# Two residual convolution layers on one core: six held chunks, a sixth tap row on PE, a first image counted from twelve buffers

## The reference

```python
# layer 0: x1 = x + conv0(gn(x))
s = z1*(1-dy)*(1-dx) + z2*(1-dy)*dx + z3*dy*(1-dx) + z4*dy*dx   # per-channel shift by under one pixel
x = x + einsum('bchw,oc->bohw', s * w_dw, w_pw)
# layer 1: out = x1 + conv1(gn(x1))
ll, lh, hl, hh = haar_dwt(x)                                     # 128x128 each
h = gelu(batchnorm(conv1x1(concatenate([ll, lh, hl, hh]), w_c1, b_c1)))   # 512 -> 128 channels
res = h
o = layernorm_chw(dwconv3x3(h, dw_w, dw_b))
o = conv1x1(gelu(conv1x1(o, pw1_w, pw1_b)), pw2_w, pw2_b)
h = gelu(batchnorm(conv1x1(o + res, w_c2, b_c2)))                # 128 -> 512 channels
out = x + haar_idwt(h)                                           # four bands back to 256x256
```

## Time and profile before

| | |
|---|---|
| median of 3 runs | 5391.47 us (5389.53 to 5392.61) |
| profiled execution | 5390.27 us, of it a span of 5388.6 us |
| busy share of the span | PE 86%, DVE 86%, ACT 80%, POOL 21% |
| counting of image 0 | 0 to 119 us |
| first pass, 8 images | 119 to 2694 us |
| c1 of image 7 | 2705 to 2822 us |
| middle | 2826 to about 4000 us |
| output | to the end |

### The profile page before, as it was taken

The page is one execution under the profiler, slowest core; times in us unless marked ns, Lnnn a source line. Parts: engine busy times, 40 slices in busy tenths (PEclk is TensorE's granted clock), DMA queues, the critical chain, the costliest instruction groups (busy, mean ns, idle before and its releaser), DMA issues.

```text
span 5388.6 us, 54861 instructions
## 1 busy us (share of the span) xinstructions
PE 4658.9 (86%) x12356; PEld 2109.0 (39%) x12356; DVE 4638.6 (86%) x4206; ACT 4333.2 (80%) x6474; POOL 1154.0 (21%) x855
## 2 busy tenths in 40 slices
PE   0889999999999999999999999999987777777775
PEld 0333334344343443444434555555642222222222
DVE  6999899898998989999808999999659888888887
ACT  4888888888788888888837888888569888888887
POOL 0000000000000000000006888888401111111111
PEclk6999999999999999999999999999999999999998
DMA  8999999999999999999973333333149999999999
GB/s 348 351 355 378 426 402 424 425 401 426 390 424 424 396 426 399 426 395 360 375 281 102 130 129 130 128 131 128 63 96 223 236 235 236 236 236 236 236 236 224
DMA packets 251726, 1562.84 MB, mean 290 GB/s; under 512 B 29744, under 2 KB 30128, under 8 KB 91824
## 3 DMA queue, kind: packets, MB, share of 16 engines
q1 hardware_dynamic: 159408, 957.11, 45.5%
q0 software_dynamic: 36864, 268.45, 24.0%
q10 hardware_dynamic: 55296, 335.57, 14.9%
HBM read 898.32 MB, written 662.70 MB: 290 GB/s over the span
## 4 chain that ended last, share of the span: by engine, by line
DMA 19%; PE 11%; DVE 10%; issue 7%; ACT 3%; POOLq 0%; DVEq 0%; POOL 0%; ACTq 0%
DMA out_x<-arena 19%; PE ps L954 4%; DVE arena L1352 3%; DVE arena L1376 2%; PE ps L880 2%; ACT arena L821 2%; PE ps L1001 2%; DVE arena L1489 2%; DVE ps L1365 2%; PE ps L961 1%; PE ps L973 1%; PE ps L985 1%; DVE arena L1481 0%; DVE arena L1480 0%; ACT arena L814 0%
## 5 line engine op out<-in xcount | busy, mean ns | idle before, releaser
L1056 PE MATMUL ps<-arena,c2T 128*128 128x512 f32 x2048 | 1025.2, 652 | 366.8 <-ACT arena L814 364.5
L880 PE MATMUL ps<-arena 128*128 128x512 f32 x2048 | 985.1, 626 | 58.7 <-DMA arena<-out_x 41.3
L864 PE MATMUL ps<-arena 128*128 128x512 f32 x2048 | 967.8, 600 | 44.6 <-DVE arena L1275 23.9
L814 ACT ACTIVATE arena<-ps,small 128x512 f32<-128x512 f32 x1024 | 713.7, 779 | 97.7 <-DVE arena L1481 90.4
L1056 PEld LDWEIGHTS ps<-arena,c2T 128*128 128x128 f32 x2048 | 401.5, 205 | 989.7 <-ACT arena L814 560.8
L859 PE MATMUL ps<-arena 128*128 128x512 f32 x1536 | 736.1, 602 | 48.3 <-DVE arena L1190 23.7
L1243 DVE SCALAR_TENSOR_TENSOR arena<-arena,shift 128x2048 f32<-128x2048 f32 x256 | 601.7, 2350 | 167.4 <-DMA arena<-in_x 117.5
L1365 DVE SCALAR_TENSOR_TENSOR ps<-arena,taps,ps 128x512 f32<-128x512 f32 (+1 forms) x604 | 686.3, 1189 | 22.1 <-PE ps L1001 21.2
L555 ACT ACTIVATE ps<-arena 128x1024 f32<-128x1024 f32 x512 | 526.4, 1028 | 164.0 <-ACT arena L587 153.1
L471 POOL TENSOR_SCALAR arena<-arena 128x256 f32<-128x256 f32 x112 | 107.2, 967 | 2525.2 <-DMA arena<-in_x 2437.3
L587 ACT ACTIVATE arena<-ps,small 128x1024 f32<-128x1024 f32 x512 | 563.7, 1101 | 102.1 <-PE ps L864 100.1
(11 more groups left out here) (168 smaller groups left out, 5869.0 us busy)
## 6 DMA issues: line engine op xcount, KB each, us to landing
arena<-in_x SPq DMA_DIRECT2D x512, 1024.0 KB, 14.7
out_x<-arena ACTq DMA_DIRECT2D x256, 1024.0 KB, 9.0
out_x<-arena POOLq DMA_DIRECT2D x256, 1024.0 KB, 17.0
arena<-out_x SPq DMA_DIRECT2D x224, 1024.0 KB, 16.7
y_dram<-arena ACTq DMA_DIRECT2D x128, 512.0 KB, 8.4
arena<-y_dram SPq DMA_DIRECT2D x128, 512.0 KB, 3.6
h_dram<-arena SPq DMA_DIRECT2D x112, 512.0 KB, 2.7
arena<-h_dram SPq DMA_DIRECT2D x112, 512.0 KB, 10.2
```

What stands on the lines that cost most here:

```text
L814: last = nc.scalar.activation(g_buf[k][:, q, :], ps[:, 4 * k + q, :], ACT.Gelu, bias=z_bias[:, q:q + 1], scale=z_scale[:, q:q + 1])
L864: last = mm(ps[:, r, :], w_center[:, :], v_buf[k][:, r * BANK:(r + 1) * BANK], start=False, stop=True, skip_group_check=True)
L880: last = mm(ps[:, 4 + s % 2, :], w_c1b[:, q, :], cells[:, q // 2, q % 2, :, :], start=(q == 0), stop=(q == 3))
L1056: last = mm(ps[:, 4 * k + q, :], c2T[:, q, :], h2[:, k * HC:(k + 1) * HC], start=True, stop=True)
```

## The change

- `HELD = 6`: besides the last group, chunks 26 and 27 of an image stay in two new buffers, `x1_more`. c1 of an image takes the four of the last group first, then those two, then chunks 0 to 25 from reloads: 26 loads where there were 28. `load_x1` and the numbers of the y1 tiles follow.
- To make room, scratch buffers are shared: `sum_x` writes its two results over the piece that it reads (in the first group of image 0 into `squares`), so its Square waits for its own Identity on a new semaphore `x_added`; `y1_squares` is a part of `squares`, so `square_x1` and `square_y1` wait for each other; the sums of y1 go to PSUM bank 6; `w_pw1b` and the raw c1 weights lie in other buffers (a copy of the first c1 block is made once); `ones` shrinks to 8 columns and the pad row is made from a broadcast column.
- `PE_ROWS = 6`: PE adds 6 of 8 rows of tap (0, 1) from tile 18 on, in two matmuls of 512 and 256 columns; DVE's part falls from 4 rows to 2.
- Image 0: its first group is loaded straight into the ring, counted there and kept; the other 28 chunks go through `ahead` and `x1_in` in turn. Six parameter loads are issued behind the first four chunks, thirteen behind the twelfth. Counting of image 1's group 0 moves from ahead of image 0's first group into that group, its group 1 into a block by itself between image 0's groups 0 and 1. Image 0's weights are made before its first group.

```diff
+HELD = 6
-PE_ROWS = TROWS // 2
+PE_ROWS = 6
+        x1_more = [cut(CH) for _ in range(HELD - SLOTS)]
+        y1_squares = squares[:, 0:BANK]
+        sums_y1 = ps[:, 6, :].rearrange("p (a n) -> p a n", a=2)
...
+        def first_chunk(g, s):
+            if g == 0:
+                return slot(s).rearrange("p r c -> p (r c)"), slot_in[s], 16
+            return (ahead[s], ahead_in[s], g * 8 + 8) if g % 2 else (x1_in[s], first_in[s], g * 8)
...
             def load_x1(b, j, s):
+                n = j * SLOTS + s
+                if isinstance(j, int) and n < HELD:
+                    return
...
+                sp.dma_start(x1_in[s], out[b, :, bass.ds((j * SLOTS + (s - HELD)) * CH, CH)]).then_inc(x1_loaded[s], 16)
...
+            def load_first_image():
+                for s in range(SLOTS):
+                    load_ring(0, 1, s)
+                    load_x_ahead(1, 1, s)
+                for s in range(SLOTS):
+                    load_x_ahead(1, 2, s)
+                with sp.Fori(2, NG - 1) as g:
+                    for s in range(SLOTS):
+                        load_ring(0, g, s)
+                        load_x_ahead(1, g + 1, s)
...
+            for t in range(NCH):
+                g, s = t // SLOTS, t % SLOTS
+                if g == 0:
+                    load_ring(0, 0, s, first=True)
+                    continue
+                if t == SLOTS:
+                    for dst, src in PARAMS:
+                        sp.dma_start(dst, src).then_inc(params_in, 16)
+                if t == 3 * SLOTS:
+                    for dst, src in LATE_PARAMS:
+                        sp.dma_start(dst, src).then_inc(late_in, 16)
+                chunk, arrived, _ = first_chunk(g, s)
+                if g > 2:
+                    wait_alone(sp, nth(t, 2 * SLOTS), x_counted, x_summed)
+                sp.dma_start(chunk, x[0, :, t * CH:(t + 1) * CH]).then_inc(arrived, 16)
...
             def sum_x(b, g, s):
-                nc.scalar.activation(x_copy, piece, ACT.Identity, accum_out=sums_x[:, 0, bass.ds(i, 1)])
-                nc.scalar.activation(x_squares, piece, ACT.Square,
+                out_ = squares[:, 0:BANK] if kept else piece
+                nc.scalar.activation(out_, piece, ACT.Identity,
+                                     accum_out=sums_x[:, 0, bass.ds(i, 1)]).then_inc(x_added, 1)
+                wait_alone(act, nth(q), x_added)
+                nc.scalar.activation(out_, piece, ACT.Square,
...
+                if first_image:
+                    for s in range(SLOTS):
+                        sum_x(1, 1, s)
...
-            for s in range(SLOTS):
-                count_x(1, 0, s)
             group_variance(1, gmom_x, ps_small_x)
             x_scales(1)
+            dve.wait_ge(late_in, 16 * len(LATE_PARAMS))
+            x_weights()
```

More of the change, by code:

```diff
@@ L21 @@
 NG = NCH // SLOTS
+HELD = 6
+ARENA = 50960
 HC = CH // 4
@@ L199, in pe_taps @@
         def pe_taps(t):
-            return [(tap, half) for tap in HEAD_PE_TAPS for half in range(2)] if t < HEAD else [(PE_TAP, 0)]
+            return [(tap, half) for tap in HEAD_PE_TAPS for half in range(2)] if t < HEAD else [(PE_TAP, half) for half in range(2)]
         def pool_taps(t):
@@ L268, in preact_kernel @@
         ahead_in = [sem(f"ahead_in{s}") for s in range(SLOTS)]
+        first_in = [sem(f"first_in{s}") for s in range(SLOTS)]
         x1_loaded = [sem(f"x1_loaded{s}") for s in range(SLOTS)]
@@ L378, in load_image @@
                         load_x_ahead(b + 1, 3, s)
-                with sp.Fori(3, NG - 1) as g:
+                for s in range(SLOTS):
+                    load_ring(b, 3, s)
+                    if before:
+                        load_x1(b - 1, 2, s)
+                    if following:
+                        load_x_ahead(b + 1, 4, s)
+                with sp.Fori(4, NG - 1) as g:
                     for s in range(SLOTS):
@@ L407, in _ @@
                 load_x1(B - 2, NG - 1, s)
-            for s in range(SLOTS):
-                load_x1(B - 1, 1, s)
-            with sp.Fori(2, NG) as j:
+            for j in range(1, 3):
+                for s in range(SLOTS):
+                    load_x1(B - 1, j, s)
+            with sp.Fori(3, NG) as j:
                 for s in range(SLOTS):
@@ L565, in x1_made @@
             def x1_made(s, place):
+                if place == "held" and s >= 2 * SLOTS - HELD:
+                    return x1_more[s - (2 * SLOTS - HELD)]
                 return x1_in[s] if place == "first" else x1_buf[s]
@@ L583, in take_x1 @@
                         act.wait_ge(c1_done, nth(b * NCH + s, NCH))
+                    if place == "held" and s >= 2 * SLOTS - HELD and not (isinstance(b, int) and b == 0):
+                        act.wait_ge(c1_done, nth(b * NCH + s, NCH + SLOTS - HELD))
                     if first and s == 0:
@@ L704, in _ @@
                 square_y1(B - 1, 0, s)
-            with act.Fori(1, NG) as g:
+            for s in range(SLOTS):
+                make_y1(B - 1, 1, s)
+                square_y1(B - 1, 1, s)
+            with act.Fori(2, NG) as g:
                 for s in range(SLOTS):
@@ L920, in _ @@
             pe.wait_ge(setup_done, 1)
-            for bank in range(7):
+            for bank in range(6):
                 last = prime(bank)
@@ L937, in _ @@
                 c1(B - 1, 0, s)
-            with pe.Fori(1, NG) as g:
+            for s in range(SLOTS):
+                c1(B - 1, 1, s)
+            with pe.Fori(2, NG) as g:
                 for s in range(SLOTS):
@@ L1134, in count_x @@
             def count_x(b, g, s, pieces=range(DVE_PIECES)):
+                chunk, arrived, count = first_chunk(g, s) if isinstance(b, int) and b == 0 else \
+                    (ahead[s], ahead_in[s], ahead_count(b, g))
                 if 0 in pieces:
-                    dve.wait_ge(ahead_in[s], b * (16 * NG) + g * 16 + 16)
+                    dve.wait_ge(arrived, count)
                 i = g * SLOTS + s
@@ L1145, in pad_row @@
             def pad_row(row):
-                return ts(ring[:, row, :], ones[:, :], pad_x, None, ALU.mult)
+                return ts(ring[:, row, :], ones[:, 0:1].broadcast_to([P, W]), pad_x, None, ALU.mult)
             def pad_columns(k):
@@ L1238, in shift_rows @@
                     done(pad_columns(1))
-                    x_weights()
+                    if not (isinstance(b, int) and b == 0):
+                        x_weights()
                 if last and s == 0:
@@ L1290, in image @@
             def image(b, before, tail, following, beyond):
+                first_image = isinstance(b, int) and b == 0
                 for s in range(SLOTS):
-                    shift_rows(b, 0, s, before, tail, (b + 1, 1) if following else None, "first")
+                    shift_rows(b, 0, s, before, tail, (b + 1, 0 if first_image else 1) if following else None, "first")
+                if first_image:
+                    for s in range(SLOTS):
+                        count_x(1, 1, s)
                 with dve.Fori(1, NG - 1) as g:
```

135 lines of the change are left out of this document (77 added, 58 removed).

## The result

The changed kernel takes 5350.1 us (median of 4 runs, 5346.32 to 5351.87), the kernel before 5391.21 on the same chip: a ratio of 0.992, 95% interval 0.991 to 0.9934. The forecast was 5349. That it fits so well is largely luck: two of the three terms came out smaller than I had them and the third more than twice as large.

The account below looks back on a forecast made before the run. The prediction took DVE to bound image 0 and the middle, ACT then DMA the later images' groups; 5390.3 - 11 (head) - 15 (first pass) - 15 (middle) = 5349 us, range 5320 to 5380.

Parts of the forecast that it names:

- Head: Start of the kernel, image 0: earlier x stream and moved counting give -11 us, bounds -18.5 to -5.
- the chunk is there 5.3 later: Block between groups 0 and 1: chunk (1,2,0) lands 5.3 us after ACT has summed (1,1,0), at 149.7.
- First pass: Images 1 to 6: two reloads fewer, less the self-wait in sum_x, give -15 us, bounds -29 to +13.
- What paces the first three is ACT: First three groups of a later image: ACT sets their pace, 39.62 us for four chunks, without real idle.
- the bound -29: First pass: best case, the saved reloads pay DMA's whole 4.9 us an image.
- now four groups stay within that: First pass: four full groups stay within the 5.7 us DMA falls behind before pacing, leaving six at ACT's pace.
- Middle: Steps with both, tiles 18 to 127: moving tap rows to PE gives -15 us, bounds -29 to +13.
- I take 7.62: PE becomes the bound: Middle step falls from 7.76 to 7.62 us, set by PE instead of DVE, over 108 steps.
- rival 1: Middle stays with DVE at 7.49 us a step, whole time 5335; chance 0.2.
- DVE waits in L1352: Middle: with PE as the bound, DVE idles ahead of L1352 in a step of 7.62 us.
- Output: Output stage: instructions and DMAs unchanged, so 0 us.
- rival 2: First pass: shared scratch lengthens ACT's group and eats the reloads' gain, whole time 5364; chance 0.16.

Follow-up runs that it names:

- Experiment 5: Changed kernel, but image 1's first group counted right after image 0, without the block between groups 0 and 1: 5334.88 us, ratio 0.9895 to the kernel before.
- experiment 4: Changed kernel, but sum_x writes its two results to separate places and ACT doesn't wait for itself there: 5349.2 us, ratio 0.992 to the kernel before.
- experiments 3 and 6: Changed kernel with four held chunks instead of six: 5355.11 us; the same also without ACT's self-wait in sum_x: 5356.11 us.
- experiment 9: Changed kernel plus three unused 1 MB copies of x an image in groups 1 and 2: 5365.22 us, ratio 0.9952 to the kernel before.
- experiment 10: Changed kernel plus three unused 1 MB copies of x an image in groups 4, 5 and 6: 5395.71 us, ratio 1.0007 to the kernel before.
- experiment 2: Changed kernel with PE making seven of the eight tap rows instead of six: 5365.38 us, ratio 0.995 to the kernel before.
- experiment 1: Changed kernel with PE's tap rows back at four of eight: 5378.4 us, ratio 0.9972 to the kernel before.

## Why the prediction came out as it did

**Head: forecast -11, measured -4.7.** The stream (17.00 for the parameters against 16.5, the last chunk landed by 88.98 against 87.2, DVE hidden under it) held to two microseconds, and yet the head's gain lies just outside its bounds (-18.5 to -5), of which the small one was kept for a slow stream. What failed is "the chunk is there 5.3 later", and which chunk it is. I took the landing time of the first load of x, when little else moved, for a load in a burst in which DMA is full: it took 13.0 and 14.7. The late chunks were those of the block itself, (1,1,2) and (1,1,3), for which ring loads stand ahead in SP's queue; I looked only at (1,2,0) behind them. Chunk (1,2,0), on which the term rested, never held DVE up, but only since the block had: it landed near 154.5, not 149.7. Experiment 5 shows the waits to be the loss. It removes the queueing and the burst together, so how much is due to each wasn't told apart.

**First pass: forecast -15, measured -3.9.** The step that failed is "What paces the first three is ACT". I read a lack of idle off ACT's timeline, whose short waits name ACT itself as the releaser, and put PE aside at 37.83 of 40 over a window in which one wait of 2.17 is all that PE lacks; over 1120 to 1175 ACT had 48.42 of 55 even before, and PE 55.00. That neither ACT's wait nor the reloads are the pace is shown by the runs; that PE is, is read from its rows, for no run made PE's work there lighter. The price of the self-wait, forecast 0.22 to 0.30 and measured 0.21 to 0.24 (0.82 to 0.85 from L673 to L676 against 0.61), was right and worth nothing (experiment 4). The reloads' 4.9 us an image were the bound -29 and were not to be had either: c1 takes the held chunks first, so the two reloads that fall away are the first of an image, in groups where DMA isn't the pace. The prices show that: 0.3 to 0.6 us for a reload there (experiments 3 and 6, 4 to 7 us over twelve), 0.8 to 0.9 for a copy there (experiment 9), 2.5 for a copy in groups 4 to 6 (experiment 10). The groups of DMA stayed at 42.4 on average where I had put ACT's 40.4; "now four groups stay within that" expected the lead of the lighter groups to last through the full ones. Why it lasts for no more than one group wasn't tried by itself. Two figures of the working don't come out either: two full groups put DMA 5.0 behind (41.8 less 39.3, twice), not 5.7, and the two groups around the end hold eight waits, of which it charged four; neither matters, as the wait cost nothing. The measured -3.9 includes +1.1 in c1 of image 7 (PE's 256 matmuls, 117.1 then 118.2), where the granted clock of PE's first 5 us was 0.67 before and 0.50 after.

**Middle: forecast -15, measured -32.9.** Both costs were right: DVE's step went to 7.49 as worked out, and PE's two passes cost 0.43. The step that failed is "I take 7.62: PE becomes the bound". From PE's 7.88 I took only 0.26 of the 0.58 of possible gaps. The loop proved elastic down to 7.53, worked out in experiment 2 from one row more, so rival 1 was the truth here: DVE keeps the middle at 7.49, with PE level. (7.76 - 7.49) x 108 is 29, the 29.3 of experiment 1: 78 of the 108 are plain steps, and the 30 at the norms gained about as much apiece, 0.3. The 3.6 that experiment 1 doesn't give back were in no term. "DVE waits in L1352" didn't come; in experiment 2, with PE at 7.74, DVE waits in its taps, L1458. The pitch of N / 2.4 + 2.5 ns of the Trainium skill ("TensorE: Matmul & The Clock Gate", Wait - 56ns, not 53.3ns?) spoke for rival 1, and its outcome held, but not its cost: the two float32 passes of 256 columns took 0.43, not 0.22. The overlap of about 93 ns that the Trainium skill gives ("ScalarE: Activation LUTs", What ACT_TABLE_LOAD costs) was too little as the price of a wait on ACT's own instruction, which took 0.21 or more, and its outcome for the pass, -29, didn't come either.

**Output:** +0.9, as good as nothing.

The sum came out since the errors of the head and the pass (6.3 and 11.1 too much) and of the middle (17.9 too little) cancel. As a forecast of the parts it was rival 1 in the middle, and nearly rival 2's time, for another reason, in the pass.

## What to carry to other kernels

Ask for each transfer that is saved in which phase it would have run: here a megabyte was worth 2.5 us where DMA was the pace and 0.3 to 0.9 where it wasn't and PE had no gap, so what to keep on chip is decided by when it would be fetched. By these prices holding two chunks that c1 wants later should give more than holding the first; that wasn't tried. An engine without idle isn't yet the pace: look for the one that is busy for the whole of a stretch, over several windows, and count its waits on others' buffers as waits. And the landing time of a load is that of its moment; a burst made by moving work together brings its own.

## What the runs showed of the hardware

A load of 1 MB that landed 5.3 us after its issue as the first load of x took 13.0 and 14.7 in a burst at 392 GB/s. A 1 MB copy within memory cost 2.5 us where DMA was full (experiment 10), as much as 1 MB comes to at the 425 GB/s of that stretch.

After the block, PE had idled 20.15 us and started at a granted clock of 0.50, the lower level of 1.2 GHz (PE's timeline and busy times of the changed kernel):

```profile
159.54 3.78 PE L936 MATMUL ps<-arena 128*128 128x512 f32 x4 [20.15 <-DVE arena L1349]
163.12 2.71 PE L941 MATMUL ps<-arena 128*128 128x512 f32 x4
```

```profile
159.50:163.10 3.60, 3.56 (x4) 1.46 (x5) 3.60 (x3) 0.00 (x0) 0.00 (x0) 0.50 0.11 46
```

Four matmuls take 3.78 there and 1.88 at a granted clock of 1.00. DVE's fused multiply-add took 485 ns for 256 columns, 760 for 512 and 1285 for 1024, so 0.21 to 0.24 us of the duration doesn't depend on the columns (an estimate from these three): a tap cut to a quarter costs 0.38 of the whole.
